# The score maxima of the first attention head pair, made during the last 18 expert tiles

## What is computed

```python
qkv = x @ w_attn                                  # 16 heads, each with 2 maps of width 8
att = softmax(where(causal, q @ k.T * scale, -inf))
att = att[:, :, 0] - lambda_full * att[:, :, 1]
out = rms_norm(att @ v) @ w_proj
...
_, idx = top_k(x @ gate_w.T, 2)                   # 8 experts, 2 for each token
out = sum over the 2 experts of c * (silu(x @ wg[e]) * (x @ wu[e])) @ wd[e]
```

## Time and profile before

| | |
|---|---|
| median of 3 runs | 3841.81 us (3839.22 to 3842.86) |
| the profiled execution's own time | 3842.5 us |
| its span | 3840.8 us |
| its mean granted TensorE clock | 0.969 |
| PE busy | 3512.2 us (91% of the span) |
| DVE / ACT / POOL busy | 2916.5 / 2234.8 / 1475.8 us |

### The profile page before, as it was taken

The page is one execution under the profiler, slowest core; times in us unless marked ns, Lnnn a source line. Parts: engine busy times, 40 slices in busy tenths (PEclk is TensorE's granted clock), DMA queues, the critical chain, the costliest instruction groups (busy, mean ns, idle before and its releaser), DMA issues. The chain is left out here.

```text
span 3840.8 us, 59450 instructions
## 1 busy us (share of the span) xinstructions
PE 3512.2 (91%) x19540; PEld 1564.0 (41%) x19541; DVE 2916.5 (76%) x4699; ACT 2234.8 (58%) x3500; POOL 1475.8 (38%) x1795
## 2 busy tenths in 40 slices
PE   8998999699999999999999998548998999989998
PEld 5555666433333333333333332413434344334344
DVE  5553222198888888888888883748999999899898
ACT  3331222137777777777777777236766666667663
POOL 1220000113333233332333333117777677676765
PEclk9999999869999999999999999869999999999999
DMA  4432111101111111111110000320000000000000
GB/s 145 159 126 78 45 45 45 43 20 31 32 32 32 32 32 32 32 29 32 32 30 29 29 28 14 129 60 1 12 11 12 12 6 17 6 12 12 6 12 6
DMA packets 119997, 143.66 MB, mean 37 GB/s; under 512 B 24184, under 2 KB 100224, under 8 KB 119728
## 3 DMA queue, kind: packets, MB, share of 16 engines
q1 hardware_dynamic: 102832, 106.69, 9.1%
q10 hardware_dynamic: 10752, 16.78, 1.3%
q0 software_dynamic: 6144, 16.79, 1.3%
HBM read 86.98 MB, written 52.43 MB: 36 GB/s over the span
## 5 line engine op out<-in xcount | busy, mean ns | idle before, releaser
L1181 DVE TENSOR_REDUCE pmax<-psR 128x1 f32<-128x512 f32 (+3 forms) x2240 | 1362.3, 669 | 201.2 <-PE psR L1231 115.2
L1122 ACT ACTIVATE prob<-psS 128x1024 f32<-128x1024 f32 (+3 forms) x1280 | 1099.5, 904 | 362.6 <-PE psS L1283 359.2
L1906 POOL TENSOR_TENSOR hc<-h_d,crep 128x512 f32<-128x512 f32 x512 | 666.4, 1306 | 370.2 <-DVE h_d L2162 223.9
L1231 PE MATMUL psR<-kslab,qslab 48*128 48x512 bf16 (+3 forms) x2560 | 719.1, 359 | 68.4 <-DMA kslab<-k_d 29.2
L1283 PE MATMUL psS<-qslab,kslab 51*128 51x512 bf16 (+3 forms) x2560 | 647.3, 352 | 4.9 <-ACT prob L1122 4.3
L1298 PE MATMUL psVo<-prob,vaug 128*32 128x512 f32 (+3 forms) x5120 | 627.0, 545 | 0.9 <-ACT ov L1126 0.9
L2370 PE MATMUL psYd<-hc,ident 128*128 128x512 f32 x1024 | 522.7, 599 | 0.3 <-POOL hc L1906 0.2
L1054 POOL TENSOR_SCALAR_AFFINE_SELECT prob<-prob 128x256 f32<-128x256 f32 (+1 forms) x512 | 208.6, 419 | 810.7 <-ACT prob L1122 810.4
L1231 PEld LDWEIGHTS psR<-kslab,qslab 48*128 48x128 bf16 x2560 | 192.9, 94 | 781.0 <-DVE pmax L1181 536.7
L2162 DVE TENSOR_TENSOR_SCAN h_d<-a,state,psU 128x512 f32<-128x512 f32 x384 | 489.2, 1274 | 0.3
L2152 DVE TENSOR_TENSOR psU<-dtx,psX 128x512 f32<-128x512 f32 x512 | 353.9, 691 | 56.5 <-POOL dtx L1894 12.7
(11 more groups left out here) (273 smaller groups left out, 4868.6 us busy)
## 6 DMA issues: line engine op xcount, KB each, us to landing
x_e<-rows_d SPq DMA_DIRECT2D x72, 128.0 KB, 2.0
y_d<-y SPq DMA_DIRECT2D x72, 128.0 KB, 1.7
q_d<-parts SPq DMA_DIRECT2D x48, 128.0 KB
k_d<-parts SPq DMA_DIRECT2D x48, 128.0 KB
qslab<-q_d SPq DMA_DIRECT2D x64, 96.0 KB
kslab<-k_d SPq DMA_DIRECT2D x64, 96.0 KB
x<-in_L_attn_x_dram SPq DMA_DIRECT2D x8, 512.0 KB, 6.1
wg<-n_L_ffn_gate_proj_w_dram ACTq DMA_DIRECT2D x8, 512.0 KB
```

The source lines that it names most:

```text
L1122: act.activation(prob[g % BUFS][:, :, off:BLK], psS[g % 2][:, :, off:BLK], ACT.Exp).then_inc(prob_ready, 1)
L1181: dve.tensor_reduce(pmax[:, a].rearrange("p i c -> p (i c)")[:, lo:lo + (count - 1) * NEXT + 1:NEXT], psR[at % BANKS][:, 0:count * w].rear ...
L1231: ins = pe.matmul(dst[:, m * w:(m + 1) * w], qslab[u][rows, i * P:(i + 1) * P], kslab[u][rows, ch * BLK:ch * BLK + w], start=(m == 0), sto ...
L1906: pool.tensor_tensor(hc[:, g % CR], h[:, g % HR], crep[:, g // PAIR % SPR], ALU.mult).then_inc(hc_ready, 1)
```

## The change

The maxima of head 0 leave `START` and are made in stage 2, four items in each of the steps 54 to 71 (`FIRST` = 54), in four slots of a step: between G and U, behind U, behind Y, and behind H. All share one new bank `psM`. A product waits until the reduction of the item before it has freed that bank (`max_free`). To make room, `psH` has one buffer in place of two. The steps from 54 on are written out. The slabs of head 0, `pmax`, `ident_b` and `mask_q` are now allocated before stage 2 and live through stage 3. POOL sets two blocks of ones and the masks at the start of stage 2, and SP loads the slabs behind tile 0. In stage 3 POOL sets six blocks of ones where it set eight, SP starts with head 1, and DVE starts with `nmax`. Two semaphores that only served one wait are folded into `lam_step`. The products, masks and reductions are the same in number and shape.

```diff
 def phase_experts(nc, io, keep, dram):
...
-        psH = ps("psH", [P, 2, MT, P])
+        psH = ps("psH", [P, MT, P])
+        psM = ps("psM", [P, BLK])
+        EACH = 4
+        FIRST = RT - (len(ITEMS) + EACH - 1) // EACH
+        FIRST -= FIRST % 2
+        def items_at(i, slot):
+            x = (i - FIRST) * EACH + slot if isinstance(i, int) else -1
+            return [x] if 0 <= x < len(ITEMS) else []
-            lo, hi = 4, RT - 2
+            lo, hi = 4, FIRST
...
-            steps(sp, step, -1, RT + 3)
+            load(0, 0)
+            sp.wait_ge(early_made, 2 + CREDIT)
+            for a in range(2):
...   # 12 transfers of head 0 as in stage 3's load()
+            steps(sp, step, 0, RT + 3)
+        @block.gpsimd
+        def _(pool):
...
+            for a in range(2):
+                c.mark(pool.memset(kslab[HALF * a + 32:HALF * a + HALF, :], 1.0))
...   # ident_b and mask_q as in stage 3 before
         def _(dve):
+            def take_max(i, slot):
+                for x in items_at(i, slot):
...
+                    dve.wait_ge(max_full, x + 1 + CREDIT)
+                    dve.tensor_reduce(pmax[...], psM[...], AX.X, ALU.max).then_inc(max_free, 1)
             def step(i, s):
+                take_max(i, 0)
+                take_max(i, 1)
...   # xT_e copy, h product
+                take_max(i, 2)
...   # y copy
+                take_max(i, 3)
         def _(pe):
+            def max_product(i, slot):
+                for x in items_at(i, slot):
...
+                    pe.wait_ge(max_free, x + 1 + CREDIT)
...   # the item's products and masks into psM
+                    ins.then_inc(max_full, 1)
...
                     for w, dst in ((keep["wg"], psG), (keep["wu"], psU)):
+                        if dst is psU:
+                            max_product(i, 0)
...
+                max_product(i, 1)
                 if known(i + 1, 0):
                     turn_x(i + 1, 1 - s)
...
+                max_product(i, 2)
...
-                    if known(i - 1, 2):
-                        pe.wait_ge(hT_ready, i - 2 + CREDIT)
+                    if known(i - 1, 1):
+                        pe.wait_ge(hT_ready, i - 1 + CREDIT)
...
+                max_product(i, 3)
 def phase_attention(nc, io, keep, dram):
...
-        START = [("max", 0, x) for x in range(NITEM)] + [("turn", 0, 0)]
+        START = [("turn", 0, 0)]
...
-            load(0)
             load(1)
...
-            for u in range(RING):
+            for u in range(1, RING):
                 for a in range(2):
...
+            whole_max(0)
             fills(START)
```

More of the change, by code:

```diff
@@ L610, in _, with score_steps, max_items @@
                 values(n)
+def score_steps():
+    out = []
+    for c in range(BPB):
+        for st in range(TPB * c + TPB):
+            r = st - TPB * c
+            first = c == 0 and st == 1
+            out.append((c, st, 0 if r < 0 or first else P * r, first))
+    return out
+def max_items():
+    diag = [tuple((i, i // TPB, P * (n + 1)) for i in range(n, ST_T, TPB)) for n in range(TPB)]
+    masked = [diag[0], diag[1][:2], diag[1][2:]] + [(one,) for group in diag[2:] for one in group]
+    full = [((i, ch, BLK),) for i in range(ST_T) for ch in range(i // TPB)]
+    order = sorted([((n + 0.5) / len(part), part is full, n) for part in (masked, full) for n in range(len(part))])
+    return [(a, (full if plain else masked)[n], not plain) for at, plain, n in order for a in range(2)]
 def phase_experts(nc, io, keep, dram):
@@ L731, in _ @@
             pe.wait_ge(keep["moe_w"], 16 * 3 * E)
+            def max_product(i, slot):
+                for x in items_at(i, slot):
+                    a, parts, masked = ITEMS[x]
+                    if x == 0:
+                        pe.wait_ge(slab_in, 192 + CREDIT)
+                        pe.wait_ge(early_made, 12 + CREDIT)
+                    pe.wait_ge(max_free, x + 1 + CREDIT)
+                    rows = slice(HALF * a, HALF * a + KM)
+                    for m, (i_, ch, w) in enumerate(parts):
+                        ins = pe.matmul(psM[:, m * w:(m + 1) * w], qslab[rows, i_ * P:(i_ + 1) * P],
+                                        kslab[rows, ch * BLK:ch * BLK + w], start=(m == 0), stop=True,
+                                        skip_group_check=True)
+                    if masked:
+                        rows = slice(HALF * a, HALF * a + HALF)
+                        dst = psM[:, 0:len(parts) * w].rearrange("p (m w) -> p m w", w=w)
+                        for part in range(2):
+                            ins = pe.matmul(dst[:, :, w - P:w], ident_b[rows, part],
+                                            mask_q[rows, part].unsqueeze(1).to_broadcast([HALF, len(parts), P]),
+                                            start=False, stop=(part == 1), skip_group_check=True)
+                    ins.then_inc(max_full, 1)
             def turn_x(i, s):
@@ L762, in step @@
                     ins.then_inc(d_done, 1)
+                max_product(i, 2)
                 if known(i - 1, 0):
                     pe.wait_ge(h_ready, i + CREDIT)
-                    if known(i - 1, 2):
-                        pe.wait_ge(hT_ready, i - 2 + CREDIT)
+                    if known(i - 1, 1):
+                        pe.wait_ge(hT_ready, i - 1 + CREDIT)
                     for m in range(MT):
-                        ins = pe.transpose(psH[:, 1 - s, m], h[:, 1 - s, m * P:(m + 1) * P], keep["ident"][:])
+                        ins = pe.transpose(psH[:, m], h[:, 1 - s, m * P:(m + 1) * P], keep["ident"][:])
                     ins.then_inc(h_turned, 1)
+                max_product(i, 3)
             steps(pe, step, -1, RT + 1)
[L773 to L791, removed]
 def phase_attention(nc, io, keep, dram):
@@ L1009, in _ @@
             c = Chain(pool, masks)
-            for u in range(RING):
+            for u in range(1, RING):
                 for a in range(2):
[L1012 to L1016, removed]
-            c.wait()
[L1018 to L1023, removed]
-                                              fill=NEG, base=HALF * part, pattern=[[-1, P]], channel_multiplier=1))
-            c.wait()
+                    c.mark(pool.memset(kslab[u][HALF * a + 32:HALF * a + HALF, :], 1.0))
+            c.wait()
+            c.after(pool.memset(fold[:], 0.0))
             for odd in range(2):
@@ L1185, in whole_max @@
             def whole_max(n):
-                for x in range(NITEM - BANKS, NITEM):
-                    freed(dve, ("max", n, x))
                 if n:
+                    for x in range(NITEM - BANKS, NITEM):
+                        freed(dve, ("max", n, x))
                     dve.wait_ge(mpart_ready, n + CREDIT)
@@ L2415, in build @@
         }
+        early = ExitStack()
         with ExitStack() as attn:
```

80 lines of the change are left out of this document (63 added, 17 removed).

## The result

| | before | changed |
|---|---|---|
| first measurement, median of 5 runs each | 3842.86 us (3839.22 to 3846.13) | 3859.98 us (3854.85 to 3865.02) |
| the changed kernel measured again | 3842.07 us (31 runs) | 3853.22 us (10 runs) |
| profiled execution: span, own time | 3840.8, 3842.5 | 3858.6, 3860.36 |

The ratio was 1.0042, 95% interval 1.0027 to 1.0057, so the change made the kernel 17.1 us, 0.4%, slower. The second measurement gave 1.0028 (1.0018 to 1.0038), 11.2 us. The forecast was 3848.7 us. The direction was right. The first measurement lies 2 us beyond the range, the second well inside.

What follows compares the result with a forecast made beforehand. PE was taken to bound stage 2 and DVE the first 42.9 us of items in stage 3. The sum -46.6 + 46.3 + 7.2 = +6.9 us gave 3848.7 us, range 3837 to 3858.

Steps and rivals of the forecast that it cites:

- The seam: Between stages 2 and 3: head 0's items and two blocks of ones go, a gain of 46.6 us.
- The rival in which the scores wait for it: Stage 3: maxima's rows land behind the slab and scores wait, up to 6 us, 3854 us; chance 0.08.
- The start of stage 2: Tile 1's load waits behind ones and slab transfers, 5.2 us; the clock's fall adds 2.0 us.
- tile 1 is not held up: Start of stage 2: slabs' tail does not delay tile 1, 2.5 in place of 7.2 us, 3844.0; chance 0.10.
- The steps: Stage 2, steps 54 to 71: four additions together 46.3 us, a step going from 5.8 to 8.4 us.
- Term 1: Steps 54 to 71: 43,008 added columns of products and masks on PE cost 17.9 us.
- Term 4: Steps 54 to 71: changes between f32 and bf16, about 0.10 us each, five a step, 9.0 us.
- type changes are free: Steps 54 to 71: number type changes alone cost nothing, 3839.7 us; chance 0.12.
- Terms 2 and 3: Steps 54 to 71: slot four's wait for `psM`, 9.2 us, and the exposed read of the expert's number, 10.2 us.
- The rival in which PE stays ahead of its queue: Stage 2's new steps: neither the number's read nor type changes show, -12.3 us, 3829.5; chance 0.12.
- the same lag, 1.7 either way: Start of the scores: the clock rises 9 us in, as before, 1.7 us either way, so no gain.
- The rival in which the clock falls within the new steps: Steps 54 to 71: gaps lower the clock, one fall in every third step is +12 us, 3861; chance 0.08.

Runs made afterwards that it cites:

- two banks, all partitions: Against the kernel with two `psM` banks: each item reads all 128 partitions instead of 48 or 64, summing both maps; 3825.88 us (0.996).
- two banks: Against the changed kernel: items alternate between two halves of `psM`, `psG` gives up one buffer; 3840.63 us (0.9994 of the kernel before).

## Why the prediction was right or wrong

**The seam**: right, -46.8 for -46.6. The first product on the slab came 22.6 us behind POOL's first block (at most 24 predicted), and the scores 10.9 us later. The side chain to `nmax` cost nothing. The rival in which the scores wait for it falls.

**The start of stage 2**: right in both parts, 5.0 and 2.0 for 5.2 and 2.0, with tile 1's turn at 325.31 (324 predicted), 1.6 of it from the kernel's start. Spreading the transfers showed the cause. The rival "tile 1 is not held up" falls.

**The steps**: 50.2 for 46.3, but the four terms are not what they were taken for. Three kernels, each with one edit more or less than the next, split them (us in 17 steps; terms 1 and 4 were predicted for all 18, in 17 they would be 17.5 and 8.5):

| kernel | 17 steps | more than the one above | term | predicted |
|---|---|---|---|---|
| before | 98.9 | | | |
| two banks, all partitions | 117.2 | 18.3 | 1, columns | 17.9 |
| two banks | 135.6 | 18.4 | 4, "type changes" | 9.0 |
| changed | 148.1 | 12.5 | 2 and 3, bank wait and read | 19.4 |

The last step, with two items, adds 1.0. Term 1 was right. **Term 4 failed**: "each change costs about 0.10", five of them a step. It was mis-sized by half, and its cause was wrong. It came from the earlier trace rows, which show the 0.10 behind an item (0.32 in place of 0.22) and 0.12 in a stretch of f32 products ahead of one, and it left out what the products further on pay. An item between f32 products pays at three places: 0.10 behind it, 0.05 to 0.10 more within the f32 products that follow (X 0.27 for 0.22), and 0.09 ahead of the item. G and U pay the last two, 1.91 for 1.72. Four items come to 1.08 a step, where the term had 0.50. (The split counts all the changes of a step in term 4, since with two banks no wait hides any; the term counted only the five outside the waits. Read off the changed kernel's rows, these are 0.83 us a step: 0.19 each for G and U, 0.10 behind each item in slots one to three, 0.05 for X and 0.10 for Y. That makes 14.1 us in 17 steps for the 8.5 predicted, and leaves 16.8 for terms 2 and 3.) And the earlier trace rows held two differences at once, the number type and 48 partitions against 128; the prediction saw only the type. Its bounds, 0 to 12.6 us, were those of the wrong mechanism, and 18.4 lies outside. The type change alone costs nothing (0.22 us in the kernel with all partitions), so the rival "type changes are free" was right on the type, and would still have missed the time. **Terms 2 and 3** were too high by 6.9 us in the split, since the changes around H fill part of the wait: slot four waited 0.26 us (H's piece of 0.85 less the 0.59 that it has with two banks), not 0.54, and the read showed 0.53 behind items of 512 columns and 0.48 on average (8.2 in 17 steps), not 0.60. The two errors nearly cancel, which is luck: with term 4 alone put right the forecast would have been 6 to 10 us higher. The exposed read itself, behind one waiting item, was as forecast, and the experiment that moves it confirms it. The rival in which PE stays ahead of its queue falls: the read showed 8.2 us and the changes 18.4. What was put at nothing held: in the kernel with all partitions X, Y and H have their old lengths, so the second read and the single buffer of `psH` cost nothing.

**The scores**: "the same lag, 1.7 either way" failed in the first execution, with 23 us at low clock for 9. The scores took 3.5 us longer, and the repeat shows that this is chance. The other 2.3 us lie behind the last score; that stretch varied from 1444.4 to 1451.4 us over the variants, which do not touch it. These 5.8 us are more than the 3.9 of the steps: the larger part of the first execution's distance from the sum is behind the first score and no step of the prediction.

**What was not foreseen**: 1.6 us at the kernel's start in this execution, 1.2 of it between PE's first product and tile 0's load, and 0.9 of that in the eight slow products. Its cause stays open.

The rival in which the clock falls within the new steps falls: it was 1.00 through all of them (630 to 790 us). The sum was +6.9; with the terms as measured and no chance in the scores it is -46.8 + 50.2 + 7.0 + 1.6 = +12.0, and the second measurement has 11.2.

## What to carry to other kernels

Before work is moved into another stage, look at what its instructions do to their neighbours there, not only at their own length: here 43,000 columns cost 18 us, and their array changes as much again. Products that use half of the partitions belong in one group, with the two halves in turn, so that they run at the same time and change the array twice for all of them; or they should use all partitions. A wait at the end of a sequence exposes whatever the engine's sequencer would have done under cover, above all reads of a register from memory; put those ahead of the wait. And large transfers that are needed 50 steps later do not belong ahead of a small one that is needed now.

## What the runs showed of the hardware

- A change between bf16 products of 48 or 64 partitions and f32 products of 128 cost 0.27 us there and back on average, at three places. f32 products of 16 partitions among f32 products of 128 showed a surcharge too (0.95, 1.05 and 0.96 us for pairs of 0.86). A change of number type alone showed nothing (0.22 us between starts at 512 columns).
- Two bf16 products of 48 partitions and 512 columns in different halves took 0.32 us together, in the same half 0.53.
- The granted clock's record showed 1.00 at the kernel's start, while eight products there took 5.2 to 6.7 us that later took 3.6, the first ones 0.85 us apart where later ones are 0.43.
- With PE busy, the clock came back 23 us behind the first score in one execution and 7 to 10 us behind it in the eleven others, one of them of the same kernel.
- A product of f32 128x128 with 128 columns took 0.22 us in two records (170 records in 19.15 us); a turn of the same size takes 0.11.
